# First-layer attention of a two-layer model: heads written out, projection in quarters, queries among the transposes

## The reference, cut to what matters

```
q = rope((x @ Wq.T).reshape(b, n, 16, 128))
k = rope(einsum('bnd,bnh->bnhd', kp, kh));  v = einsum('bnd,bnh->bnhd', vp, vh)
p = softmax(where(tril, einsum('bnhd,bmhd->bhnm', q, k) / sqrt(128), -inf))
attn = einsum('bhnm,bmhd->bnhd', p, v).reshape(b, n, 2048) @ Wout.T
x = x + attn + moe(xn)          # xn: x normalised; then layer 1 in the same way
```

## Time and profile before

| | us |
|---|---|
| device time, median of 3 runs | 1444.87 (1433.82 to 1458.12) |
| span of the profiled execution | 1350.4 (its own device time is not recorded) |
| TensorE / VectorE / ScalarE / GpSimd busy in it | 1196.7 / 831.6 / 495.8 / 501.8 |
| mean granted clock of TensorE | 0.929 |

### The profile page before, as it was taken

One profiled execution on the slowest core, in us unless ns is written; L12 is line 12 of the kernel. 1 busy time (PEld: TensorE's weight loads), 2 busy tenths in 40 slices (PEclk: granted clock), 3 DMA queues, 4 the chain that ended last, 5 costly groups with the idle time before them and its releaser, 6 DMA issues. The chain is left out here.

```text
span 1350.4 us, 23037 instructions
## 1 busy us (share of the span) xinstructions
PE 1196.7 (89%) x5610; PEld 847.0 (63%) x5613; DVE 831.6 (62%) x2066; ACT 495.8 (37%) x1468; POOL 501.8 (37%) x479
## 2 busy tenths in 40 slices
PE   6669999999849999779999888795989989999895
PEld 5446668666648777556668655575544468888442
DVE  4968882788205555389992899824844434544486
ACT  2335551555203333335551444403113323333331
POOL 0657672577000000066672555403267200000575
PEclk9879999999979999889999999997996789999697
DMA  9432221223354555422221122002049034454343
GB/s 363 175 94 90 88 88 39 65 87 102 160 117 149 159 155 159 128 87 78 79 90 39 59 69 73 25 0 74 31 159 399 34 98 155 157 156 153 92 135 113
DMA packets 107065, 154.49 MB, mean 114 GB/s; under 512 B 13713, under 2 KB 87697, under 8 KB 104721
## 3 DMA queue, kind: packets, MB, share of 16 engines
q1 hardware_dynamic: 67072, 95.07, 21.9%
q0 software_dynamic: 12288, 33.57, 7.8%
q10 hardware_dynamic: 27648, 25.18, 5.3%
HBM read 97.01 MB, written 56.75 MB: 114 GB/s over the span
## 5 line engine op out<-in xcount | busy, mean ns | idle before, releaser
L1066 ACT ACTIVATE probs<-bank,negmax 128x512 f32<-128x512 f32 (+3 forms) x256 | 134.3, 537 | 195.3 <-DVE negmax L966 173.4
L812 POOL TENSOR_TENSOR parts<-wq,parts 128x256 fp32r<-128x256 f32 x64 | 50.0, 781 | 376.9 <-ACT parts L1058 376.9
L1263 DVE COPY probsT<-bank 128x256 f32<-128x256 f32 x192 | 81.5, 425 | 175.3 <-PE bank L1175 175.3
L1191 PE MATMUL bank<-big_a,probsT 128*128 x768 | 183.5, 362 | 0.6 <-DVE probsT L1263 0.2
L901 PE MATMUL bank<-probsT,big_b 128*128 128x512 f32 (+3 forms) x512 | 156.8, 450 | 21.8 <-ACT probsT L1079 21.7
L875 PE MATMUL bank<-kT,qT 128*128 128x512 f32 (+3 forms) x512 | 172.5, 459 | 1.2 <-ACT probs L1066 1.2
L1191 PEld LDWEIGHTS bank<-big_a,probsT 128*128 128x128 f32 x768 | 141.6, 194 | 22.9 <-issue 8.8
L901 PEld LDWEIGHTS bank<-probsT,big_b 128*128 128x128 f32 x512 | 93.6, 192 | 95.3 <-issue 49.5
L1505 POOL DMA_INDIRECT big_a<-ys_dram,slot_r x64 | 62.7, 979 | 223.8 <-POOLq L146 204.6
L862 PE MATMUL bank<-parts 128*128 128x512 f32 x384 | 110.9, 426 | 19.6 <-POOL parts L812 15.0
L966 DVE TENSOR_REDUCE negmax<-bank 128x1 f32<-128x512 f32 (+3 forms) x256 | 109.9, 484 | 13.7 <-PE bank L877 11.6
(11 more groups left out here) (194 smaller groups left out, 2023.9 us busy)
## 6 DMA issues: line engine op xcount, KB each, us to landing
probs<-xs_dram SPq DMA_DIRECT2D x192, 128.0 KB, 2.1
ys_dram<-work ACTq DMA_DIRECT2D x192, 128.0 KB, 1.7
work<-khT_dram SPq DMA_DIRECT2D x64, 256.0 KB, 3.1
xs_dram<-big_a SPq DMA_DIRECT2D x12, 1024.0 KB, 19.5
wq<-in_wq SPq DMA_DIRECT2D x64, 128.0 KB, 2.1
big_a<-in_gu SPq DMA_DIRECT2D x1, 8192.0 KB, 25.0
big_a<-in_gu SPq DMA_DIRECT2D x1, 6144.0 KB, 18.5
big_b<-in_dn SPq DMA_DIRECT2D x1, 4096.0 KB, 36.2
```

What stands on the lines that cost most here:

```text
L1066: nc.scalar.activation(s.probs[:, par, ROW_AT[i]:ROW_AT[i] + (i + 1) * P], s.ps[bank][:, at:at + (i + 1) * P], ACT.Exp, bias=s.negmax[:, p ...
L1191: mm = nc.tensor.matmul(s.ps[2 + j % 2][:, 0:W], rowsT[:, j % 2, k * P:(k + 1) * P], gu[:, k, bass.ds(e * W, W)], start=k == 0, stop=k == ...
L1263: v.tensor_copy(rowsT[:, j % 2, :], s.ps[j % 2][:, 0:EMB]).then_inc(rowsT_ready, 1)
```

## The change

The heads are written out, with no hardware loop. In TensorE's step the transposes of u - 1 and the six query matmuls of u + 2 become one sequence (`turn_and_query`), and in the second batch four heads' worth of one row tile of the first batch's projection is put in between (`project_quarter`: row tile i in heads 16 + 4i to 19 + 4i, bank 5). `oT` has a buffer for each batch. The last batch's projection uses a bank for each row tile; its first 15 heads of row tile 0 are multiplied before the last values. VectorE adds a finished row tile after `normalise`. The score order is 1, 3, 2, 0, and TensorE waits for the exponentials of one bank at a time. The transposed group 2 moves from bank 5 to bank 2. ScalarE evicts all four groups, and each group's values matmul waits for its own eviction only. The low part of the second batch's input is formed in head 1 before the rotation, and lies over `xnT` in place. The load of `gu0` waits for the first batch's projection too, since the new `oT` buffer lies under it.

```diff
-    s.oT = s.big_a[:, 48 * 256:80 * 256].rearrange("p (h n) -> p h n", h=H0)
+    s.oT = [s.big_a[:, at * 256:(at + 32) * 256].rearrange("p (h n) -> p h n", h=H0) for at in (16, 48)]
+ORDER0 = (1, 3, 2, 0)
+SCORED0 = {1: 1, 3: 2, 2: 4, 0: 4}
+FREED0 = {1: 1, 3: 2, 2: 4}
+TURN_BANK0 = [(3, 0), (4, 0), (2, 256), (4, 384)]
+TURN_ORDER = (0, 1, 3, 2)
+TURNED0 = {0: 1, 1: 3, 3: 3, 2: 4}
+QUERY_AFTER = {2: 0, 4: 1, 6: 2, 7: 3, 9: 4, 10: 5}
+LAST_BANKS = (5, 3, 4, 0)
...
             if extra == "scatter":
                 sp.wait_ge(q_done, NU)
+                sp.wait_ge(wout_done, ROWS * (len(rows) - 1))
                 sp.dma_start(s.gu0, ...)
...
# TensorE
-                if not (isinstance(u, int) and u == 0):
-                    pe.wait_ge(exped, ROWS * u)
-                for i in ORDER:
+                for i in ORDER0:
+                    if u and i in FREED0:
+                        pe.wait_ge(exped, ROWS * (u - 1) + FREED0[i])
+                    if u >= 2 and i == 1:
+                        pe.wait_ge(out_a, ROWS * (u - 1))
...
+            def turn_and_query(u, ahead):
+                par, n = u % 2, 0
                 pe.wait_ge(prob_ready, ROWS * u + ROWS)
+                if u:
+                    pe.wait_ge(out_a, ROWS * u)
+                for j in TURN_ORDER:
+                    bank, at = TURN_BANK0[j]
+                    if j == 2 and u + 1 < NU:
+                        pe.wait_ge(exped, ROWS * (u + 1) + 1)
                     for i in range(j, ROWS):
                         mm = nc.tensor.transpose(...)
+                        if i == ROWS - 1:
+                            mm.then_inc(turned, 1)
+                        n += 1
+                        if ahead < NU and n in QUERY_AFTER:
+                            if QUERY_AFTER[n] == 0:
+                                query_waits(ahead)
+                            query_term(ahead, QUERY_AFTER[n])
...
-                pe.wait_ge(out_v, u + 1)
-                pe.wait_ge(out_a, (ROWS - 1) * (u + 1))
-                for j in range(ROWS):
+                for n, j in enumerate(TURN_ORDER):
+                    pe.wait_ge(out_a, ROWS * u + n + 1)
...
+            def project_quarter(u):
+                bi, i, q = u // H0 - 1, u % H0 // 4, u % 4
+                pe.wait_ge(o_ready, H0 * bi + 4 * q + 4)
+                if q == 0 and i:
+                    pe.wait_ge(x_added, added_at["out", bi, i - 1])
+                elif q == 0 and bi:
+                    pe.wait_ge(x_added, added_at["out", bi - 1, ROWS - 1])
+                project(bi, i, range(4 * q, 4 * q + 4), 5)
...
+            for u in range(NU):
+                scores(u)
+                ...
+                turn_and_query(u - 1, u + 2)
+                if u >= H0:
+                    project_quarter(u)
+                values(u - 1)
+            bi = len(rows) - 1
+            turn_and_query(NU - 1, NU)
+            pe.wait_ge(o_ready, NU - 1)
+            project(bi, 0, range(H0 - 1), LAST_BANKS[0])
+            values(NU - 1)
+            for i in range(1, ROWS):
+                project(bi, i, range(H0 - 1), LAST_BANKS[i])
+                if i == 1:
+                    pe.wait_ge(o_ready, NU)
+                    project(bi, 0, (H0 - 1,), LAST_BANKS[0])
+                project(bi, i, (H0 - 1,), LAST_BANKS[i])
...
# VectorE
-            heads(dve, step, project, lambda: out0(NU - 1, len(rows) - 1, H0 - 1))
+            for u in range(NU):
+                maxima(u)
+                if combining:
+                    for k in (2 * (u % 2), 2 * (u % 2) + 1):
+                        combine(u // 2, k)
+                if u == 1:
+                    for bi in range(1, len(rows)):
+                        low_of_x(bi)
+                if u + 2 < NU:
+                    rotate(u + 2)
+                normalise(u)
+                if u >= H0 and u % 4 == 3:
+                    add_out(u // H0 - 1, u % H0 // 4, 5)
...
# ScalarE, outs(u)
-                for n, j in enumerate((1, 3, 2)):
+                for j in TURN_ORDER:
+                    act.wait_ge(turned, ROWS * u + TURNED0[j])
```

More of the change, by code:

```diff
@@ L770, in wout_count @@
[L770 to L782 removed]
         @block.sync
         def _(sp):
[L786 to L788 removed]
+            wq = d["wq0"].rearrange("(h k p) n -> p h k n", k=KC, p=P)
@@ L903, in values @@
                 mm.then_inc(weighted, 1)
-            def step(u, bi, h, par):
-                scores(u, par)
-                first = isinstance(u, int) and u == 0
-                if isinstance(h, int) and h == 1 and bi:
-                    pe.wait_ge(x_added, wout_count(bi - 1, ROWS - 1))
-                if not first:
-                    turn(u - 1, 1 - par)
-                ahead = next_row(bi, h)
-                if ahead is not None:
-                    query(u + 2, ahead, par)
-                if not first:
-                    values(u - 1, bi - 1 if isinstance(h, int) and h == 0 else bi)
@@ L934, in drain, with project @@
-            def drain():
-                u = NU - 1
-                turn(u, 1)
-                values(u, len(rows) - 1)
-            query(0, 0, 0)
-            query(1, 0, 1)
-            heads(pe, step, project, drain)
+            def project(bi, i, heads, bank):
+                for h in heads:
+                    mm = nc.tensor.matmul(s.ps[bank][:, 0:EMB], s.oT[bi][:, h, i * P:(i + 1) * P], s.wout[:, h, :],
+                                          start=h == 0, stop=h == H0 - 1)
+                if H0 - 1 in heads:
+                    mm.then_inc(wout_done, 1)
@@ L1015, in statistics, with add_out @@
+            def add_out(bi, i, bank):
+                t = rows[bi] * ROWS + i
+                dve.wait_ge(wout_done, ROWS * bi + i + 1)
+                if added_before(("out", bi, i)):
+                    dve.wait_ge(x_added, added_before(("out", bi, i)))
+                v.tensor_tensor(s.x[:, t, :], s.ps[bank][:, 0:EMB], s.x[:, t, :], ALU.add).then_inc(x_added, 1)
             def statistics(tiles):
@@ new lines, in _ @@
+            last = len(rows) - 1
+            if combining:
+                dve.wait_ge(x_added, added_at["out", last, 0] - 1)
+                statistics(range(TILES - ROWS))
+            for i in range(ROWS):
+                add_out(last, i, LAST_BANKS[i])
+                if combining and i:
+                    dve.wait_ge(x_added, added_at["out", last, i - 1])
+                    statistics([TILES - ROWS + i - 1])
+            if combining:
+                dve.wait_ge(x_added, added_at["out", last, ROWS - 1])
+                statistics([TILES - 1])
+                for t in range(TILES):
+                    dve.wait_ge(stat, t + 1)
+                    v.bn_aggr(s.meanvar[:, t, :], s.stats[:, t, :]).then_inc(aggr, 1)
```

330 lines of the change are left out of this document (129 added, 201 removed).

## The result

| us | before | after |
|---|---|---|
| device time, same chip, median | 1439.34 of 4 runs (1432.46 to 1458.12) | 1400.46 of 4 runs (1400.1 to 1405.6) |
| ratio, 95% interval | | 0.9757 [0.9715, 0.9799] |
| span of the profiled execution | 1350.4 | 1398.2 |
| mean granted clock | 0.929 | 0.913 |

A forecast was written before the change was run, and what follows sets the result against it. TensorE was taken to bound the first block and the second's first batch, VectorE its second batch. Gains of 11.3 + 41.7 = 53.0 us, less 3 for collisions, gave 1444.87 - 50 = 1395 us; range 1376 to 1424.

The forecast's parts named there:

- (a): First-layer attention: projection quarters dealt to the next batch's heads, 8.99 us each; second batches gain 7.1 and 30.1 us.
- (c): First-layer heads: new score order, waits by bank and by single eviction remove about 0.2 us a head before the values.
- I leave 3 us for collisions that remain in the first batch: Deduction from the summed gain of 53.0 us for VectorE and GpSimd meeting in the first batch; one costs 2 to 3.
- rival A: Second block's first batch: VectorE and GpSimd collisions stay, 8.7 us a head, 18 us more, 1413 us; chance 0.12.
- (b): First-layer heads: first eviction moved to ScalarE, hidden there; VectorE gets 0.7 us a head, its combines precede the key product.
- Carrying 94.5 us over: Difference between the profiled span, 1350.4 us, and the timed median, 1444.87, taken as lying around the span and unchanged.
- (d): First-layer heads: query matmuls placed between the transposes; taken as zero, with ±12 us kept for the range.
- (e): First-layer attention loops written out: taken as worth nothing.
- rival E: Written-out heads: instructions arrive late, 2.1 us in each of 40 heads, 84 us, 1479 us; chance 0.03.
- (f): Second batch's low part formed before head 3's rotation: 2.5 us gained at the second block's start, none in the first.
- (g): First layer's expert weights, loaded after the first batch's projection, need 18.5 us and end some 15 us before use.
- (h): Block ends: projection's first 15 heads fill the wait for the last values; 38.9 us against 40.8 and 40.9.

The follow-up runs named there:

- e5: The kernel after, unchanged, run again on the second chip: 1305.15 us beside 1352.25 of the kernel before.
- e7: The kernel before with GpSimd's key product of the next head put before the scatters or gathers: 1320.2 us, ratio 0.9823.
- e9: The kernel before with its two first-layer attention hardware loops written out and nothing else: 1321.65 us, ratio 0.9801.
- e3: The kernel after with the first batch's projection in one piece again, after the values of head 15: 1321.04 us, ratio 0.9839.
- e6: The kernel after with the first batch's projection in one piece and GpSimd's key product before the scatters or gathers: 1308.72 us, ratio 0.9702.
- e2: The kernel after with GpSimd's key product of the next head put before the scatters or gathers: 1288.57 us, ratio 0.9578.
- e8: The kernel after with the eviction of the first transposed group back on VectorE: 1304.39 us, ratio 0.9678.
- e1: The kernel before, unchanged, profiled again together with its own device time: 1357.55 us, ratio 0.9952.
- e4: The kernel after with the six query matmuls behind the ten transposes again: 1307.86 us, ratio 0.9749.
- e10: The kernel after, but the values matmuls wait for all four evictions before the first of them: 1328.69 us, ratio 0.9893.
- e12: The kernel after, unchanged, run six times on the third chip: 1304.93 us beside 1352.86 of the kernel before.

## Why the prediction was right, and which step was wrong

The median came at 1400, 5 above the forecast, and where layer 1 is undisturbed the span came at 1304.6 (e5) against 1300.4. Both are closer than the steps deserve, and that is luck. The gain was 39 us and not 50; half of that miss vanished because the median of before, with a fourth run, fell from 1444.87 to 1439.34. One term of the sum was off by 17 us, and a gain that was in no step made up for most of it on the second and third chips.

**Length of a head, steps (a) and (c): right.** Scores are 7.21 apart in block 1's first batch (forecast 7.27). TensorE's timeline of one head:

```profile
170.78 0.59 PE L854 MATMUL bank<-kT,qT 128*128 128x256 f32 x2
...
173.33 0.39 PE L870 MATMUL bank<-const,probs 128*128 128x128 f32 x2
173.47 0.48 PE L838 MATMUL bank<-parts 128*128 128x512 f32 x1
...
175.84 2.32 PE L886 MATMUL bank<-probsT,big_b 128*128 128x512 f32 x8
178.00 0.59 PE L854 MATMUL bank<-kT,qT 128*128 128x256 f32 x2
```

The joint before the values, 0.21 us idle in the earlier trace rows, is gone. In the second batches they are 8.95 apart (forecast 8.99): 132.7 and 134.3 us against 133.4 forecast.

**Where the 30 us of step (a) come from: the size was right, the reason only in part.** 163.5 became 134.3. But e7 and e9 reach 141 with the projection in one piece, by an even pace alone. On top of an even pace the quarters give 5.2 us (e3, block 1) to 7.7 (e6 against e2). In one piece the seam costs 27.9 us of TensorE, and the quarters take as much of it: work that is dealt out is not hidden while TensorE is the bound. The prediction saw that the 120.7 of 127.7 us of VectorE were stretched by the meeting, but set out to hide them behind TensorE; that undoing the meeting itself gives 22 of the 30 us (e7) was not looked at.

**The step that failed: "I leave 3 us for collisions that remain in the first batch".** The stretch took 114.3 us against 94.5, 19.8 more: that is rival A, priced at 18 us and given 0.12. It was weighed down by step (b), by which 0.7 us less on VectorE "sets its combines before the key product instead of on it". e8 shows the opposite: the combines are moved further onto the product (2.27 us against 1.61), and the stretch is as long with that eviction back on VectorE (113.7). e2 shows what decides: with the same work on both engines in another order it is 96.4. And e3 shows that the same code has both paces, so that less work on VectorE could not rule one out; so A should have been the likelier case and not one in eight: the slow pace is in all three profiles of the kernel after. Of 10 timed runs of the kernel after on the second and third chips 2 are at 1281 and 1283 and 8 at 1303.7 to 1309.2; the medians of the two groups are 23 us apart, about the 20 us by which the two paces differ. That the two runs had the even pace is argued: no profile fell on one.

What the collisions cost: from the even pace of e3 to the slow one of the kernel after, four rows of normalising go from 1.74 to 2.65 us and two combines from 1.06 to 2.27, 2.1 us in all. VectorE had some 0.5 us of idle time in a head, and the other 1.6 are the way from 7.21 to 8.80 a head. In the Trainium skill, SBUF — State Buffer, section SBUF: two separate sides, the port pair shared by the two engines is locked for a whole instruction. By that rule the trace agrees again: the delay of the combines, 1.21 us, is near the length of the key product that they meet, 1.29. In three other kernels the product was already running when the combines started, and their delay follows what was left of it: 0.73 us left and 0.55 late in e8, 0.77 and 0.58 in e2, 1.00 and 0.86 in the kernel before. The prediction put that last delay at nearly the whole 1.29.

**Carrying 94.5 us over: wrong, and harmless.** 2.3 us lie around a span (1398.2 and 1400.5; 1350.2 and 1352.4). A difference taken over is right whatever the constant is, as long as both kernels bear it. Two small things in the sums are harmless too: added up from its own rows, VectorE's head with every collision is 9.6 us and not 9.4 before, and 8.9 and not 8.8 in step (a), because the rows of a timeline overlap by some 0.1 us; 8.9 is still under 8.99.

**The gain that was in no step.** On the second chip 47 us were gained, and the blocks show less: the end of block 2 moves from 913.6 to 881.8, 31.8 us. The other 14 us are in the rest, 436.8 to 422.8, code that is the same. They lie in the first attention block of layer 1. Stretches from 56 us behind block 2's end on in e1, with the granted clock in the third column from the right, and the last four of them in e2:

```profile
970.84:1004.84 34.00, 31.52 (x114) 18.51 (x112) 17.10 (x26) 1.79 (x3) 22.49 (x23) 1.00 0.26 93
1004.84:1017.84 13.00, 11.28 (x26) 4.69 (x27) 4.91 (x13) 5.09 (x14) 8.96 (x10) 0.59 0.94 381
1017.84:1029.84 12.00, 12.00 (x34) 6.29 (x33) 6.65 (x17) 5.16 (x19) 9.25 (x10) 0.50 0.99 422
1029.84:1041.84 12.00, 12.00 (x36) 5.45 (x35) 3.92 (x10) 3.30 (x11) 9.26 (x10) 0.66 0.95 374
1041.84:1053.84 12.00, 12.00 (x37) 5.50 (x36) 4.21 (x11) 3.31 (x11) 9.17 (x10) 0.72 0.62 237
1053.84:1065.84 12.00, 12.00 (x38) 5.75 (x36) 4.84 (x13) 4.68 (x14) 2.92 (x3) 0.69 0.12 44
```

```profile
965.51:977.51 12.00, 12.00 (x35) 6.55 (x35) 6.48 (x17) 5.41 (x20) 9.26 (x10) 0.50 1.00 426
977.51:989.51 12.00, 12.00 (x47) 5.34 (x46) 4.88 (x12) 3.85 (x13) 9.26 (x10) 0.96 0.95 373
989.51:1001.51 12.00, 12.00 (x54) 5.68 (x53) 7.73 (x19) 5.97 (x21) 8.95 (x11) 1.00 0.62 236
1001.51:1013.51 12.00, 12.00 (x59) 6.86 (x58) 7.27 (x17) 5.46 (x20) 2.77 (x3) 1.00 0.12 44
```

TensorE had been busy 31.5 of 34 us at the full clock before it fell. In both kernels it is then at the lower of its two levels (0.50, 1.2 GHz) for twelve microseconds, in which TensorE is never idle. In e2 it is back at the upper level (0.96 in the next stretch, then 1.00, 2.4 GHz) and stays there; in e1 it is granted in part of each later stretch only (0.66 to 0.72), and TensorE gets through 36 to 38 matmul records in twelve microseconds instead of 47 to 59. The rest (table above) of before, e1, e3 and e6 (435 to 437 us) has the first form, that of e2, e4, e5, e7, e10 and e12 (423 to 426) the second, e9 (428.5) is between. The difference is 12 to 14 us. e6's four runs lie in two pairs 12 to 13 us apart, and before's 18 runs on the second and third chips in two groups, 1337 to 1342 and 1351 to 1361, that differ by as much; on the first chip its 23 runs spread from 1337 to 1365 with a few between. What decides it was not tried; that the changed kernel falls on the better side by more than luck is open, as e3 and e6, which hold most of the change, fall on the other.

**The sum by its terms**, in the profiled executions of before and after, both counted from the first scores matmul of a head:

| term | forecast | measured |
|---|---|---|
| block 1, heads 3 to 15 | 2.3 | 3.0 |
| block 1, heads 16 to 31 | 7.1 | 7.8 |
| block 2, heads 3 to 15 | 7.1, less 3 | -12.7 |
| block 2, heads 16 to 31 | 30.1 | 29.2 |
| both ends | 3.9 | 4.6 |
| start of block 1 | 0 | -0.3 |
| start of block 2 | 2.5 | 2.5 |
| both blocks together | 50.0 | 34.1 |

From head 3 to the last matmul, forecast at about 267 us in both blocks, block 1 took 265.1 and block 2 287.2.

**(b) Wrong**, as above. **(d) Right** at zero; e4. **(e) Right** that fetching costs nothing, and rival E is out: no unreleased idle time appeared on TensorE, and the instruction queues carried 0.87 MB instead of 0.68:

```profile
q8 instruction: 35, 0.57, 0.2%
q14 instruction: 37, 0.30, 0.1%
```

Wrong that writing the loops out does nothing: e9 is 31 us faster, 27 of them through the pace. **(f) Not shown.** The start of block 2, heads 0 to 2, took 24.3 to 30.6 us over all kernels, and 28.7 in before but 24.6 in e1, which is the same kernel; the 2.5 us in the table are within that, and that they equal the forecast is luck. The wait of 2.48 us that the step was priced by the earlier trace rows is 0.64 in e1. The 4.06 us of the values in that row, against 2.4 elsewhere, are another thing again: the granted clock was 0.57 from 603.5 to 607.4.

**(g) Right.** SyncE issues the expert weights at 337.96, 5.6 us after the scores of the last head began (forecast 5.3), and the load has its 33 us of cover; the first transpose of the expert tiles had waited 3.43 us before, now 3.34:

```profile
374.29 1.36 PE L1147 MATMUL bank<-const,probs 128*128 128x128 f32 x4 [3.34 <-DMA probs<-xs_dram]
```

**(h) Right**, 38.6 us from the first scores against 38.9: the first 15 heads' part of the projection stands before the last values, and no gap is left:

```profile
341.00 6.64 PE L892 MATMUL bank<-big_b,big_a 128*128 128x256 f32 x30
347.48 2.32 PE L886 MATMUL bank<-probsT,big_b 128*128 128x512 f32 x8
349.63 21.32 PE L892 MATMUL bank<-big_b,big_a 128*128 128x256 f32 x98
```

**Rival C** (interleaving gives 0.2 us a head) is out by e4. **Rivals D** (waits that cost 0.21 each) **and F** (quarters that stand alone) are out by the stretches of block 1, 93.77 and 132.70 us, in which TensorE is busy from end to end.

## What to carry to other kernels

When one code shows two paces in one profile, ask first where two engines meet that slow each other, and move one instruction of the cheaper engine: here that is worth 19 us for one product moved on GpSimd, and it takes the chance out of the rest (4 runs within 0.6 us). Taking work off the slowed engine is no substitute: it moves the meeting, and here to a longer one (e8). A busy share near one on an engine whose instructions run longer than in the next stretch is no proof that it has too much work: compare the mean length of each kind first, and only then the shares. And before a difference of spans is put down to a change, the stretches whose code is the same must be taken off; here they gave 14 us of 47 on one chip and hid as much as 82 in a single profile.

## What was not expected of the hardware

**Long stops beside indirect transfers on one chip.** In the kernel after's layer 1, in the profile with 519.1 us, VectorE's maxima stood idle for 6 to 25 us at a time, with scores that TensorE had finished long before. The last rows of TensorE's timeline before the longest stop, VectorE's, and GpSimd's within it:

```profile
1311.20 0.29 PE L1494 MATMUL bank<-maskb,identb 128*128 128x128 bf16 x1
```

```profile
1294.89 0.76 DVE L1555 TENSOR_REDUCE negmax<-bank 128x1 f32<-128x384 f32 x2 [14.71 <-DMA probs<-in_sd]
...
1344.70 1.68 DVE L1555 TENSOR_REDUCE negmax<-bank 128x1 f32<-128x512 f32 x4 [25.18 <-DMA probs<-in_sd]
```

```profile
1334.40 0.95 POOL L1477 DMA_INDIRECT big_a<-ys_dram,slot_r  x1 [0.30 <-issue]
```

Such stops lie where GpSimd issues its indirect transfers in a row, here 64 from 1254.7 to 1334.4, one each 1.26 us; TensorE and ScalarE have stops of up to 25 and 27 us in the same places, and the longest of VectorE's reaches 10 us beyond the last issue. The releaser named is an old transfer, and taken not to be the cause. On the three other chips the same code takes 96 us less (422.8 in e5, 425.7 in e12, 423.5 in e4), with the same row of issues, one each 1.29 us in e5, and none of VectorE's stops beside them. Whether it is late signals or late instructions is open, and so is whether the transfers have a part in it: no experiment fell on that chip.

**The clock in layer 1**, as shown above: for one code, 36 us at 0.66 to 0.72 (e1) or at 0.96 to 1.00 (e2), and 12 to 14 us between them.
